# Five identity multiplications on TensorE ahead of the scaled keys' transposes, in the first phase of a decoder layer

## The reference, cut to what matters

```
h  = layernorm(x)
q, k, v = silu(conv4(h @ Wq)), silu(conv4(h @ Wk)), silu(conv4(h @ Wv))   # causal, 4 taps
beta = sigmoid(h @ Wb)
q, k = l2norm(q), l2norm(k);  kb = k * beta         # per head, 4 heads of 64
inv  = -(kb @ k.T) * strict_lower                    # per chunk of 32 tokens, then substitution
short, long = conv5(v), conv64(v)                    # causal, per channel
...                                                  # delta rule, gates, output, attention, feed-forward
```

## Time and profile before

| | |
|---|---|
| three runs, us | 1267.31, 1263.83, 1260.26; median 1263.83 |
| profiled execution | 1260.86 us, of which the span is 1259.1 |
| busy over the span | PE 1084.3, PEld 793.7, DVE 984.7, ACT 755.2, POOL 645.1 us |
| mean granted clock | 0.949 |
| phase 1 | 0 to 248 us |

### The profile page before, as it was taken

One profiled execution on the slowest core, in us unless ns is written; L12 is line 12 of the kernel. 1 busy time (PEld: TensorE's weight loads), 2 busy tenths in 40 slices (PEclk: granted clock), 3 DMA queues, 4 the chain that ended last, 5 costly groups with the idle time before them and its releaser, 6 DMA issues. The chain is left out here.

```text
span 1259.1 us, 28322 instructions
## 1 busy us (share of the span) xinstructions
PE 1084.3 (86%) x8715; PEld 793.7 (63%) x8799; DVE 984.7 (78%) x2955; ACT 755.2 (60%) x1456; POOL 645.1 (51%) x2360
## 2 busy tenths in 40 slices
PE   5798988596788989999999999999999977875755
PEld 4677767494456666777777677677777744542224
DVE  4899989696776887988888888898888778624975
ACT  5787878533344456666666766766666553435766
POOL 4777776415356564665656555565565644001006
PEclk9988988798899999999999999999999998897979
DMA  5666766546224254334335435434532532115006
GB/s 163 212 206 199 229 197 184 188 123 169 80 68 122 82 138 140 92 108 148 95 114 149 119 117 149 126 107 124 149 93 81 161 97 61 43 40 187 1 7 227
DMA packets 159830, 160.33 MB, mean 127 GB/s; under 512 B 65320, under 2 KB 126656, under 8 KB 159680
## 3 DMA queue, kind: packets, MB, share of 16 engines
q1 hardware_dynamic: 155552, 157.47, 41.6%
q10 hardware_dynamic: 4128, 1.05, 0.4%
HBM read 96.34 MB, written 61.87 MB: 126 GB/s over the span
## 5 line engine op out<-in xcount | busy, mean ns | idle before, releaser
L2154 DVE CUSTOM_DVE_ANT_0 x_psA<-x_psA,x_mask_q 128x256 f32<-128x256 f32 x496 | 200.6, 446 | 60.0 <-PE x_psA L1438 59.1
L1706 ACT ACTIVATE x_PT<-x_psB 128x512 f32<-128x512 f32 x240 | 143.6, 598 | 143.1 <-PE x_psB L1465 141.8
L314 DVE SCALAR_TENSOR_TENSOR a_conv<-a_ps_proj,taps,a_conv 128x253 f32<-128x253 f32 (+2 forms) x288 | 115.0, 470 | 16.7 <-ACT a_conv L381 16.7
L537 PE MATMUL a_ps_proj<-a_hT,wqkv 128*128 128x256 f32 x384 | 108.4, 432 | 9.5 <-DVE a_conv L314 6.6
L1438 PE MATMUL x_psA<-x_Ks,x_Qs 96*128 96x256 bf16 x496 | 97.6, 278 | 15.5 <-DVE x_maxima L2154 13.3
L1465 PE MATMUL x_psB<-x_Qs,x_Ks 98*128 98x256 bf16 x480 | 93.0, 274 | 10.5 <-issue 5.9
L537 PEld LDWEIGHTS a_ps_proj<-a_hT,wqkv 128*128 128x128 f32 x384 | 80.0, 219 | 29.7 <-issue 14.6
L2154 DVE DVE_READ_ACCUMULATOR2_ANT x_maxima<- 128x1 f32 x512 | 72.0, 141 | 0.0
L1479 PE MATMUL x_psO<-x_PT,x_V 128*32 128x256 f32 x1024 | 71.1, 397 | 0.7 <-ACT x_PT L1706 0.7
L2377 POOL TENSOR_TENSOR f_y<-f_y,f_x 128x512 f32<-128x512 f32 x16 | 22.9, 1454 | 87.8 <-DVE f_y L2365 80.2
L1465 PEld LDWEIGHTS x_psB<-x_Qs,x_Ks 98*128 98x128 bf16 x480 | 47.6, 99 | 32.0 <-issue 1.4
(11 more groups left out here) (385 smaller groups left out, 3256.7 us busy)
## 6 DMA issues: line engine op xcount, KB each, us to landing
scratch_keypack<-a_keypack SPq DMA_DIRECT2D x16, 768.0 KB, 3.8
c_keypack<-scratch_keypack SPq DMA_DIRECT2D x16, 768.0 KB, 4.6
x_Ks<-scratch_k_parts SPq DMA_DIRECT2D x192, 64.0 KB, 2.4
matrix<-scratch_taps_copies SPq DMA_DIRECT2D x32, 256.0 KB, 4.0
scratch_k_parts<-x_parts_k SPq DMA_DIRECT2D x32, 192.0 KB, 2.3
scratch_q_parts<-x_parts_q SPq DMA_DIRECT2D x32, 192.0 KB, 2.5
x_Qs<-scratch_q_parts SPq DMA_DIRECT2D x32, 192.0 KB, 2.9
a_x_in<-in_x SPq DMA_DIRECT2D x16, 256.0 KB, 3.7
```

The source lines that it names most:

```text
L314: nc.vector.scalar_tensor_tensor(acc, ps_proj[PROJ_BANK[p]][:, c, 0:L - j], taps[:, p, c, TAPS - 1 - j:TAPS - j], acc, ALU.mult, ALU.add). ...
L537: last = nc.tensor.matmul(ps_proj[PROJ_BANK[p]][:, o], wqkv[:, p, c, o * P:(o + 1) * P], hT[par][:, c], start=c == 0, stop=c == FC - 1)
L1706: nc.scalar.activation(PT[:, k % (2 * GROUP)], bank_B(b, k)[0], ACT.Exp, scale=XD ** -0.5).then_inc(pexp_ready, 1)
L2154: last = nc.vector.tensor_tensor_reduce(bank_A(b, k)[0][:, s], bank_A(b, k)[0][:, s], mask_q[:, t], 1.0, LOWEST, ALU.add, ALU.max, maxima[ ...
```

## The change

For each batch, before `ksT` waits for the scaled keys, TensorE multiplies the identity with itself five times: the 128 x 128 float32 identity read as bfloat16 gives 128 x 256 values; 128 columns of them are the weights, and the whole, read twice, is a moving operand of 512 columns. The product goes into the whole bank `ps_tok[0]`, which the transposes of `ksT` then overwrite. For this the wait for `squared[0]` (the bank is free) is moved ahead of the five, and the wait for `ks_ready` follows them. No other engine's instructions change.

```diff
--- before.py
+++ after.py
@@ -83,6 +83,7 @@
 
 W_LOADS = 16 * 9
 FIR_COLS = P + HB
+A_HOT = 5
 COPIES = 16
 COPY_PARTS = 4
 STEP = P // COPIES
@@ -502,6 +503,7 @@
         @block.tensor
         def _(pe):
             pe.wait_ge(ident_loaded, 16)
+            pair = ident[:].bitcast(BF16)
 
             def part(op, b):
                 par = b % 2
@@ -559,8 +561,11 @@
                             last = nc.tensor.transpose(ps_tok[1][:, t, c * P:(c + 1) * P], shortT[:, c, t * P:(t + 1) * P], ident[:])
                     last.then_inc(short_turned, 1)
                 elif op == "ksT":
+                    after(b, (squared[0], 1, 1), (keypack_ready, -1, 1))
+                    for _ in range(A_HOT):
+                        nc.tensor.matmul(ps_tok[0][:].rearrange("p t n -> p (t n)"), pair[:, 0:P],
+                                         pair.unsqueeze(1).broadcast_to([P, 2, L]), start=True, stop=True)
                     pe.wait_ge(ks_ready, b + 1)
-                    after(b, (squared[0], 1, 1), (keypack_ready, -1, 1))
                     for c in range(FC):
                         for t in range(TT):
                             last = nc.tensor.transpose(ps_tok[0][:, c, t * P:(t + 1) * P], ks_tok[:, t, c * P:(c + 1) * P], ident[:])
```

## The result

The changed kernel took 1257.67 us (median of 15 runs, 1251.31 to 1266.64), the kernel before 1264.85 us on the same chip (15 runs, 1258.71 to 1270.86). The ratio is 0.9948, 95% interval 0.9926 to 0.9971. I had forecast no measurable change, at 1265 in a range of 1258 to 1275. The time came out just under the range, and it fell by 0.3 to 0.7% where my sum had it rise slightly: wrong.

A forecast was written before the change was run, and what follows sets the result against it. POOL's own instructions were taken to pace phase 1's steady turns. 1260.86 (profiled execution) + 1.3 (held turns) + 0.8 (end) = 1263.0 us; with the median 3.0 us above that execution, at most 1266, forecast 1265, range 1258 to 1275.

The forecast's parts named there:

- The cover of 1.7 us: Steady turns: DVE finishes `norms` 1.7 us before POOL's `norm` starts, so the five delay nothing there; price 0.
- the term for held turns: Turns where `short1` holds a small POOL instruction over 2 us: one more than the profile's two, +1.3 us.
- Gain in the length of a turn: 0: Steady turns: TensorE gains 1.7 us, but POOL sets the length, so 0 if POOL's instructions last as long.
- POOL is disturbed less: Rival, steady turns: earlier DVE work falls into POOL's gaps, up to 1.1 us a turn; 1256 us, chance 0.10.
- the end, "+0.8": End of phase 1: the second to last `ksT` waits behind the five, 1.2 us, less 0.4 at the last batch.
- the -0.4: Last batch: its five lie in a wait of 3.01 us and may bring `ksT` from 1.12 to 0.71 us.

The follow-up runs named there:

- `tail` on ACT: Kernel before with POOL's `tail` instruction (1.03 us) given to ACT as two activations: ratio 0.9882 to the kernel before, 1250.0 us against 1265.2.

## Why the prediction was wrong

**Right.** What the page and the earlier trace rows were read for: `ksT`'s wait is slack behind POOL, the five fit into it (1.25 us measured, 1.23 foreseen), the full clock comes, `proj_q` takes 1.89 us, DVE's idle time shrinks, and TensorE ends up waiting for the same `ks`. POOL as the pace is shown by `tail` on ACT. The moved wait costs nothing that shows. The cover of 1.7 us behind the five held in the steady turns, where POOL waits for nobody; the turns of 14.0 us in the kernel before, and one of 13.85 in the changed kernel's second trace, in both of which POOL waits some 0.5 us for `norms`, show that it can be used up where TensorE comes late.

**Wrong: the term for held turns, "I take one more than now, +1.3".** I took the two full-clock turns of the profile for samples of what the change makes. They are the first full-clock turns after a slow one (or after the filling of the pipeline), with `short1` at 6.5 and 7.0 us. When every turn is fast, DVE is ahead of its work and `short1` starts at 6.13, where nothing was held in any of 43 turns, in four traces with the five in them. So a held turn belongs to where DVE stands, and a low clock in the turn before is one way to bring it there; another turn of that kind, with `short1` at 6.41 in the kernel before's second trace, was not held, and with `tail` on ACT held turns came at the full clock too. In the trace that the sum was made against, one held turn of two goes away, -1.3 us where I had +1.3. The second trace of the kernel before has none to lose.

**Wrong, and the step that failed: "Gain in the length of a turn: 0".** I had made that depend on POOL's own instructions lasting as long as before, and they did not. I had the mechanism as the rival "POOL is disturbed less", with its two places (0.2 us at L63, 0.5 us at the copy), and gave it 0.10 and up to 0.55 us a turn, since "a moved overlap stays an overlap". It moved from an overlap of 1.16 us a turn in POOL to one of 0.87: 0.3 us a turn, over ten turns 3 us. The rival's name was right and its size half of what I had priced.

**Not confirmed: the end, "+0.8".** The 1.2 us in the path at batch 14 are there, but the end as a whole did not get longer: 40.7, 42.3 and 41.5 us from the thirteenth `ks` to the next phase in the changed kernel, 43.2 and 41.3 before. I had no term for the projection of v, which stands in the chain there and takes 3.06 us at the low clock, 1.97 at the full one. It differs between traces of both kernels (3.06 and 3.39 before; 1.97, 3.16 and 2.52 after), so no gain of the change can be booked on it. The last batch's `ksT` takes 0.70, 1.12 and 0.65 us in the changed kernel's three traces, so the -0.4 that I had for it comes in two of them.

**The sum again**, over traces: turns 1 to 12 take 162.5 us before (two traces) and 159.7 after (three), -2.8; the end -0.8; together -3.6, of a measured -6.6 (3.7 to 9.4 by the interval) and, on the other chip, -5.2 (2.0 to 8.3). The held turns and the 14.0 us turns vary between executions, and two traces, 164.6 and 160.4 us, sample them poorly; the surest part is the 0.3 us of a turn at the full clock against an ordinary one. Whether the rest, 1.6 to 3 us, is in them or in the later phases is open; those take 1009.4 to 1017.9 us in the changed kernel's traces and 1010.9 and 1012.9 before, which doesn't decide it.

I also took the profiled execution, 3.0 us under the median, for typical of the turns. It was one with two held turns of twelve, and its sibling had none.

## What to carry to other kernels

Where one engine paces a loop with its own instructions, a faster neighbour can still change its speed, by moving the moments at which the two meet at a shared port; add up the pacing engine's durations in each kind of turn, and the difference is the gain. A turn that follows another kind of turn is no sample of a steady state: look at where each engine stands at its start. A filler that holds the clock should stay shorter than the gap (2.34 us here): it paid with five, 1.25 us, and nothing was left with twelve, 2.76 us.

## What the runs showed of the hardware

Six DVE instructions over SBUF, 2.44 us, held one small POOL instruction through all of them (2.34 to 2.55 us), or put off several POOL instructions by a part of a DVE instruction each (0.31 to 0.55 us, where they take some 0.2 alone). The kernel before did either with `short1` 6.98 us after `ks`: one was held in the first turn of its first trace, none in the ninth of its second. So that distance alone does not decide it. With `short1` at 6.47 to 6.49 us in a steady turn one was held all six times, in three traces. DVE was put off too: beside a `ks` of 1.38 us its instruction took 1.02 us, not 0.18. The Trainium skill ("SBUF — State Buffer", section "SBUF: two separate sides") says that the two engines share a port pair, held for one instruction. The trace shows more: a POOL instruction that is put off through six.

Transposes of float32 in the gap kept TensorE at 2.4 GHz as well as bfloat16 multiplications of 512 columns (clock 1.00 from 50 to 200 us). The Trainium skill ("TensorE: Matmul & The Clock Gate", section "Part 4: PE-mode transpose") says, beside a measurement with bfloat16, that the full clock doesn't engage for transposes; here, with float32 and between the kernel's other multiplications, it stayed.
